# Pairing the score banks of the first attention: one exponential of 1024 columns for two heads, and three banks for the maxima

## What is computed

```python
h = layernorm(layernorm(x)) * ln_gamma + ln_beta      # the first call is the outer norm
q, k, v = heads(h @ w_qkv + b_qkv)                    # 16 heads of 8 dimensions, T = 1024
attn = softmax(q @ k.T / sqrt(8))
x = x + (layernorm(x) + heads_joined(attn @ v) @ w_out + b_out)
```

## Time and profile before

| | |
|---|---|
| runs | 2936.1, 2939.1, 2948.2 us; median 2939.1 us |
| profiled execution | 2946.5 us, span 2944.7 us |
| busy over the span | PE 93%, DVE 79%, ACT 72%, POOL 61% |
| first attention | about 24 us (first maxima) to 861 us (last sums) |
| busy from 400 to 500 us | PE 92.8, DVE 87.2, ACT 76.3, POOL 29.1 us |
| granted TensorE clock | 1.00 of full speed from 92.6 to 826.4 us, 0.50 from 51.6 to 92.6 us and from 826.4 to 853.7 us |

### The profile page before, as it was taken

One profiled execution on the slowest core, in us unless ns is written; L12 is line 12 of the kernel. 1 busy time (PEld: TensorE's weight loads), 2 busy tenths in 40 slices (PEclk: granted clock), 3 DMA queues, 4 the chain that ended last, 5 costly groups with the idle time before them and its releaser, 6 DMA issues.

```text
span 2944.7 us, 46590 instructions
## 1 busy us (share of the span) xinstructions
PE 2752.8 (93%) x16447; PEld 2032.8 (69%) x16447; DVE 2317.6 (79%) x4143; ACT 2126.2 (72%) x4692; POOL 1801.3 (61%) x1357
## 2 busy tenths in 40 slices
PE   6999999999899999999999999999999999999996
PEld 3333333333347777788888888888888888888885
DVE  8888888888937877789788777777777778777876
ACT  2677777777766555677877777777777787777773
POOL 3442524332015555677788777788778787777773
PEclk8899999999989999999999999999999999999997
DMA  1000000000022111000000000000000000000000
GB/s 41 7 7 7 12 7 7 7 7 2 2 76 75 48 48 58 8 1 1 1 1 3 3 1 3 3 1 3 3 1 3 3 1 3 3 1 3 3 3 6
DMA packets 25689, 34.83 MB, mean 12 GB/s; under 512 B 4136, under 2 KB 14952, under 8 KB 25456
## 3 DMA queue, kind: packets, MB, share of 16 engines
q1 hardware_dynamic: 25456, 31.85, 3.4%
HBM read 29.08 MB, written 2.23 MB: 11 GB/s over the span
## 4 chain that ended last, share of the span: by engine, by line
PE 67%; DVE 15%; ACT 8%; issue 6%; POOL 5%; DMA 0%; DVEq 0%; POOLq 0%; ACTq 0%
PE P L1798 18%; PE P L1666 9%; PE P L1825 8%; PE P L1809 6%; PE P L1651 5%; PE P L1727 5%; PE P L1639 4%; ACT a_PT L784 4%; DVE c_nm L1376 4%; DVE c_DT L1401 3%; PE P L1781 3%; PE P L1738 2%; PE P L1835 2%; PE P L1629 2%; POOL d_tn L1099 2%
## 5 line engine op out<-in xcount | busy, mean ns | idle before, releaser
L1376 DVE TENSOR_REDUCE c_nm<-P 128x1 f32<-128x1024 f32 x512 | 624.4, 1220 | 303.9 <-PE P L1798 301.9
L908 ACT ACTIVATE c_P<-P,c_nm 128x1024 f32<-128x1024 f32 x512 | 573.0, 1119 | 251.8 <-DVE c_nm L1376 247.5
L1221 DVE TENSOR_REDUCE a_mx<-P 128x1 f32<-128x512 f32 x1024 | 640.2, 683 | 99.5 <-PE P L1639 95.4
L784 ACT ACTIVATE a_PT<-P 128x512 f32<-128x512 f32 x1024 | 537.1, 603 | 165.4 <-PE P L1651 165.2
L2048 POOL TENSOR_TENSOR c_P<-c_P,c_P 128x1024 f32<-128x1024 f32 (+1 forms) x256 | 623.0, 2434 | 21.3
L2046 POOL TENSOR_SCALAR c_P<-c_P,c_rr 128x1024 f32<-128x1024 f32 (+1 forms) x256 | 300.9, 1176 | 338.4 <-DVE c_rr L1388 338.4
L1825 PE MATMUL P<-c_DT,c_xkh 128*128 128x256 f32 x2048 | 451.7, 283 | 24.7 <-DVE c_Yl L1409 23.0
L1651 PE MATMUL P<-a_Qs,a_Ks 32*128 32x512 f32 x1024 | 344.2, 493 | 59.6 <-ACT a_PT L784 53.2
L1825 PEld LDWEIGHTS P<-c_DT,c_xkh 128*128 128x128 f32 x2048 | 350.2, 189 | 37.0 <-DVE c_Yl L1409 29.2
L1798 PE MATMUL P<-c_xth,c_Th 128*128 128x512 f32 x1024 | 365.1, 437 | 2.8 <-ACT c_P L908 2.8
L1401 DVE TENSOR_TENSOR c_DT<-P,c_DT 128x512 fp32r<-128x512 f32 x512 | 348.4, 681 | 9.0 <-ACT c_DT L919 8.8
(11 more groups left out here) (245 smaller groups left out, 5393.6 us busy)
## 6 DMA issues: line engine op xcount, KB each, us to landing
b_cwB<-cw_scratch SPq DMA_DIRECT2D x64, 256.0 KB, 5.0
c_stg<-in_cw SPq DMA_DIRECT2D x8, 640.0 KB, 4.0
a_Qs<-a_mT SPq DMA_DIRECT2D x256, 2.0 KB
b_stg<-in_moe SPq DMA_DIRECT2D x9, 384.0 KB, 3.0
out<-xres SPq DMA_DIRECT2D x15, 128.0 KB, 1.8
xres<-in_x SPq DMA_DIRECT2D x3, 512.0 KB, 7.6
xres<-in_x SPq DMA_DIRECT2D x2, 256.0 KB, 3.0
a_hTl_f<-in_wqk SPq DMA_DIRECT2D x1, 512.0 KB, 3.6
```

The lines of the kernel that those rows point to most:

```text
L784: e.activation(m.PT[j][hs % 4][:, :], bank("scores", u, hs, j), ACT.Exp, scale=SCALE).then_inc(m.S["a_exp"])
L908: e.activation(m.P1[s][n % 4][:, :], P[:, k:k + 2, :].rearrange("p c k -> p (c k)"), ACT.Exp, bias=m.nm[:, n % 4, s:s + 1], accum_out=m.sm ...
L1221: e.tensor_reduce(m.mx2[u % 2][:, t // 4, j, t % 4, half:half + 1], bank("maxima", u, t, j, half), AX, ALU.max).then_inc(m.S["a_max_dve"])
L1376: e.tensor_reduce(m.nm[:, n % 4, s:s + 1], P[:, k:k + 2, :].rearrange("p c k -> p (c k)"), AX, ALU.max, negate=True).then_inc(m.S["c_nm"])
```

## The change

Scores are computed in pairs. `scores(u, hs, k)` stands for two heads, (2, 3) for k = 0 and (0, 1) for k = 1, into two neighbouring banks, and one exponential of 1024 columns reads both. The pairs of banks are (4, 5) and (6, 7), in turn; the maxima ring loses bank 3, which now holds the sums. A group is now M0 S(2,3) M1 sums M2 S(0,1) M3. The steps in `RINGED_ACT` take a whole pair, except that the two halves of a projection share one; for this they now stand together at slot 3 instead of slot 1, and `out_project` moves from slot 5 to slot 6.

```diff
-    ring = Ring([0, 1, 2, 3])
-    act_ring = Ring([5, 6, 7])
+    ring = Ring([0, 1, 2])
+    score_pairs = Ring([(4, 5), (6, 7)])
...
-        if step[0] in RINGED_ACT:
-            p.on([act_ring.take()], *step)
+        if step[0] == "project" and step[1]:
+
+            p.on([p.bank["project", *step[1:3], 0] + 1 if step[3] else score_pairs.take()[0]], *step)
+        elif step[0] in RINGED_ACT and score_pairs:
+            p.on(score_pairs.take(), *step)
...
-                hook(s0 + 3 - w, 1, "project", u + 1, w, c)
+                hook(s0 + 3 - w, 3, "project", u + 1, w, c)
...
-                hook(e0 + 7 + 4 * r, 5, "out_project", b, r)
+                hook(e0 + 7 + 4 * r, 6, "out_project", b, r)
...
-            if 0 <= ue < NU:
-                p.on([act_ring.take()], "scores", ue, m_e, (i + 2) % 4)
+            if i % 2 == 0 and 0 <= ue < NU:
+                p.on(score_pairs.take(), "scores", ue, m_e, i % 4 // 2)
...
-                    p.on([4], "sums", up, m_p)
+                    p.on([3], "sums", up, m_p)
...
-    m.PT = [[sb(f"a_PT{j}_{i}", [128, 512]) for i in range(4)] for j in range(4)]
+    m.PT = [[sb(f"a_PT{j}_{i}", [128, 2, 512]) for i in range(4)] for j in range(2)]
...
-        e.activation(m.PT[j][hs % 4][:, :], bank("scores", u, hs, j), ACT.Exp, scale=SCALE).then_inc(m.S["a_exp"])
+        e.activation(m.PT[SCORE_HEADS[k][0] // 2][hs % 4][:, :, :], P[:, first:first + 2, :], ACT.Exp, scale=SCALE).then_inc(m.S["a_exp"])
...
+        for i, j in enumerate(SCORE_HEADS[k]):
+            r = slice(32 * j, 32 * j + 32)
+            tt = e.matmul(P[:, first + i, :], m.Ks[u % 3][r, 128 * kt:128 * kt + 128],
+                          m.Qs[u % 3][r, 512 * c:512 * c + 512], start=True, stop=True)
+        tt.then_inc(m.S["a_st"])
```

More of the change, by code:

```diff
@@ L21 @@
 LAG0 = 7
+SCORE_HEADS = ((2, 3), (0, 1))
 NE, NI = 9, 256
@@ L379, in plan_all @@
     p.do("load_cw", 0, 1)
-    ring.slots, ring.i, act_ring = [7], 0, ring
+    ring.slots, ring.i, score_pairs = [7], 0, None
     pairs = Ring([(0, 1), (2, 3), (4, 5)])
@@ L778, in row2, with scores @@
         e.activation(t[:, 1, :].bitcast(F32), ps[0:16, 0:128], ACT.Copy).then_inc(m.S["a_mt_act"])
-    def scores(u, hs, j):
-        w.wait_ge(*at("a_st", "scores", u, hs, j))
+    def scores(u, hs, k):
+        first = v.plan.bank["scores", u, hs, k]
+        w.wait_ge(*at("a_st", "scores", u, hs, k))
         if 16 * u + hs > 3:
             w.wait_ge(*at("a_pv", "sums", *divmod(16 * u + hs - 4, 16)))
-        e.activation(m.PT[j][hs % 4][:, :], bank("scores", u, hs, j), ACT.Exp, scale=SCALE).then_inc(m.S["a_exp"])
+        e.activation(m.PT[SCORE_HEADS[k][0] // 2][hs % 4][:, :, :], P[:, first:first + 2, :], ACT.Exp, scale=SCALE).then_inc(m.S["a_exp"])
     def sums(u, hs):
@@ L791, in sums @@
                 w.wait_ge(*at("a_ot_pe", "divide", u - 1, c))
-            e.activation(m.OT[:, 512 * c:512 * c + 512], P[:, 4, :], ACT.Copy).then_inc(m.S["a_oe"])
+            e.activation(m.OT[:, 512 * c:512 * c + 512], P[:, 3, :], ACT.Copy).then_inc(m.S["a_oe"])
     def turn_o(b, r):
@@ L1645, in row2, with scores @@
         e.transpose(ps[0:16, 0:128], m.nm0[u % 2][c][:, :], ident).then_inc(m.S["a_mt_pe"])
-    def scores(u, hs, j):
+    def scores(u, hs, k):
         c, kt = divmod(hs, 8)
-        ps, r = bank("scores", u, hs, j), slice(32 * j, 32 * j + 32)
+        bank("scores", u, hs, k)
+        first = v.plan.bank["scores", u, hs, k]
         w.wait_ge(*at(f"a_mdma{u % 3}_{c}", "row2_low", u, c))
-        e.matmul(ps, m.Ks[u % 3][r, 128 * kt:128 * kt + 128], m.Qs[u % 3][r, 512 * c:512 * c + 512],
-                 start=True, stop=True).then_inc(m.S["a_st"])
+        for i, j in enumerate(SCORE_HEADS[k]):
[3 more added lines that the diff above has]
+        tt.then_inc(m.S["a_st"])
     def sums(u, hs):
@@ L1656, in sums @@
         c, kt = divmod(hs, 8)
-        O = P[:, 4, :]
+        O = P[:, 3, :]
         for j in range(4):
             at_v = 144 * kt + 9 * (4 * gr + j)
-            w.wait_ge(*at("a_exp", "scores", u, hs, j))
+            w.wait_ge(*at("a_exp", "scores", u, hs, 1 if j < 2 else 0))
             w.wait_ge(*at("a_v_dve", "values", b, 1))
@@ L1665, in sums @@
                 w.wait_ge(*at("a_oe", "sums", u - 1, 15))
-            tt = e.matmul(O[32 * j:32 * j + 32, :], m.Vp[b % 2][:, at_v:at_v + 32], m.PT[j][hs % 4][:, :],
+            tt = e.matmul(O[32 * j:32 * j + 32, :], m.Vp[b % 2][:, at_v:at_v + 32], m.PT[j // 2][hs % 4][:, j % 2, :],
                           start=(kt == 0), stop=(kt == 7))
```

## The result

The changed kernel takes 2983.1 us in the median of 20 runs (2946.9 to 3034.8), the kernel before 2948.1 in 20 runs beside it (2936.1 to 2959.9). So the change is slower, by 0.8% at least, and 2983 lies outside my range of 2914 to 2951. It is near the 2991 of rival C.

What follows compares the result with a forecast made beforehand. The bound was taken as the loop through ACT and three score banks, 0.2 us over DVE. Terms 8.1 - 24.4 + 11.6 + 5 + 5 - 12 + 1 = -5.7, from the runs' median, gave 2933 us; range 2914 to 2951.

Steps and rivals of the forecast that it cites:

- rival C: Main stage: TensorE's clock falls as the new plain period leaves it waiting 0.6 us; slower, 2991 us; chance 0.06.
- The plain period: Main stage's ordinary periods: maxima loop through three banks makes each 2.70 us instead of 2.64; +8.1 us over 131.
- Projections: 27 periods with two projections: 3.44 us instead of 4.34, as the next scores take the other pair; -24.4 us.
- row2 and divide: 26 periods with both: row2 takes a pair, next scores wait for an exponential; 4.10 us, not 3.65; +11.6 us.
- P: Rival theory in the experiments: the plain period of three banks itself lets the clock fall; no chance given.
- The second half of C: After a fall in the main stage, plain periods cost 4.16 us, not 2.70, until the next projections.
- The other hooks: Periods with turn_h, values or out_project, and those behind turn_h: together +5 us, bounds 0 to +8.
- Side work: DVE's statistics and aggregations for the norms, no longer hidden because the new loop runs through DVE: +5 us.
- The tail: Periods without maxima at the end: two pairs and no third bank to wait for, so shorter periods; -12 us.
- The head: Start of the kernel: maxima alone keep DVE's pace; half-clock periods with scores 4.16 against 4.09, four times; +1 us.
- The base: Starting time for the sum: profiled execution of 2946.5 us, with the median of the runs shown 7.4 lower.

Runs made afterwards that it cites:

- old_three_banks: The kernel before with one change, a maxima ring of three banks instead of four (bank 3 unused): 2971.0 us, ratio 1.0087 to the kernel before.

## Why the prediction was wrong

*The plain period* (+8.1): right. 2.70 us through the third bank, shown alone in old_three_banks at 0.064 a period.

*Projections* (-24.4): the size right, 3.49 for 3.44, the reason mostly wrong. Three quarters of it comes without pairs. POOL does not bind; its bad bound of -12 can go.

*row2 and divide* (+11.6): the length right, 4.09 for 4.10. **This is the step that failed.** "The next S(2,3) waits for the exponential of S(0,1), just started": I priced that wait as the 0.45 us by which it lengthens 26 periods, and did not ask what TensorE does in it. In most of them it does nothing, for 0.45 to 0.64 us in one piece, and behind some of them the clock falls: five times in the fastest run, at some 13 us, and more in the others, by 0.39 us for each microsecond at the lower level. Taken away (2920), filled (2930), put into the other kernel (3015) and filled there (2962), it answers each time.

*Rival C* (0.06): the right kind of mechanism at the right price, 4.16 us for a plain period at the lower level, in the wrong place. I held the plain period's wait to be 0.6 us and dismissed C by the tail's periods of 2.60, which kept the clock; for plain periods that was right, and P did fall. It was silent on the row2 periods, for which I asked no row, though my own step before it had just made their wait. The second half of C holds in part: plain periods of 4.16 kept the clock low for up to 51 us with the row2 period among them, and it came back in projections at 352.6, 393.6 and 598.4; but at 182.0 and 741.8 it came back in plain periods. The Trainium skill (TensorE: Matmul & The Clock Gate, section "A second HAM failure mode: psum-queue depth-cycling") tells of a clock that goes up and down in a kernel that cycles through PSUM banks, with short idle times between its groups of matmuls. The direction agrees with the 0.96 of this trace; but old_three_banks cycles through its banks with such idle times too and stays at 1.00, so they are not enough by themselves.

*The other hooks* (+5): +3.6. *Side work* (+5): +0.7, perhaps because DVE caught up in the next period; no run tests that. *The tail* (-12): -14 in the profile. *The head* (+1): +3.8, and +5.9 with three banks in the kernel before. Where maxima run alone, from about 56 us on, all three kernels take 0.60 us for each, as I held; the time is lost before 56 us, among the projections of the first units. The base was off as well: my 2939.1 was the median of three runs, and twenty gave 2948.1. And the busy shares that I gave for 94 to 806 us are those of 400 to 500; over the whole stretch they are 92%, 87% and 78%, which changes nothing in the sum.

What stays open: why one row2 period brings the clock down and the next of the same form does not, which makes the time of a run a matter of where the falls come; why pauses as long or longer in plain and turn_h periods did not; and what in old_three_banks makes its tail low for 44 us.

## What to carry to other kernels

Price an added wait twice: by how much it lengthens the period, and by what TensorE does in it; if that is nothing, move the step behind the work that needs no wait, or fill the gap. Put a side step where the loop has just been fed, and try that before rebuilding its buffers: three slots and a tail's banks gave 1.5% here, with none of the pairs. And compare the clock of all runs, since one profile can be the luckiest of twenty.

## What the runs showed of the hardware

A pause of 0.45 to 0.66 us on TensorE, in a period of 4.1 us or more in which it is busy on both sides, was in some cases (5 of 24 in the changed kernel's trace) followed by 3.4 to 51 us at the lower level. Pauses of 0.42 to 0.55 us in plain periods, and of 0.88 us in six periods with turn_h, were followed by none, so the length of a pause did not decide it. Three unneeded matmuls, 0.96 us in each period with row2, took the low clock out of the main stage in two different kernels. An exponential of 1024 columns took 1.02 us against 2 x 0.60, and merging two was worth nothing where the loop did not wait for ACT. And the clock's record in a trace can begin late: in old_three_banks it reads 1.00 up to 98.4 us, over matmuls of the length of the lower level.
